# A transformer block with routed and shared experts: the shared network's operands fetched in the stage before, and its down products two chunks behind

## The chip, the cores and the metric

The kernel runs on one core of a Trainium2 chip. The metric is the device time of one execution, in microseconds (us); lower is better.

## What is computed

One block over x of 4 x 2048 tokens of width 256: attention, then a network of 8 routed experts (two for each token) beside a shared one. Everything is float32. The part that the change touches:

```python
y = jnp.einsum('te,etd->td', combine, expert_out)   # the two chosen experts, weighted
return y + _swiglu_mlp(identity, sw_gate, sw_up, sw_down)
# _swiglu_mlp: silu(x @ wg) * (x @ wu) @ wd, 256 -> 704 -> 256
```

and around it `x = x + gb * ffn(h)`, with h the normalized and modulated x (in the kernel: h2), and x itself before the addition (in the kernel: x1).

## The kernel before

The program is a row of stages, each with a block of instructions for every engine and a barrier at its end: setup, qkv, attention, middle (residual, norm, routing, rows scattered to the experts), expert, shared. The engines are TensorE (PE), VectorE (DVE), ScalarE (ACT), GpSimd (POOL) and SyncE (SP), which issues most DMAs; each works its list in order and waits on semaphores.

Products are made in fp32r with operands split in two: a high part (an ACT copy) and a low part (a subtraction, operand minus high part), and three products high-high, high-low, low-high.

**The expert stage** takes 39 blocks of 512 rows. For each it loads the expert's weights and the rows, transposes and splits them, makes three chunks of 128 hidden columns and adds them up in the down products; DVE copies the result (`take_made`, tile `made`, L1850) and SP stores it in `expert_made` (L1738). At its end SP waits for the last store.

**The shared stage** (`shared_stage`) loads the shared weights in five DMAs (L2008 to L2012), splits them (ACT L2096, DVE L2174), then walks 16 units of 512 tokens, unrolled. A unit has six chunks (NC = 6) of hidden columns; the sixth holds 64 columns of gate and, in the same product, 64 of up. For chunk i:

- PE: `up` (L2191) makes gate and up products, 12 matmuls of 512 columns, 6 for the last chunk. It needs the silu and `hid_f` of chunk i-2, whose PSUM it takes over. Then `down` (L2202), 12 matmuls of 256 columns, for the chunk before.
- ACT: silu (`act_g`, L2086, L2088). Behind that of chunk 2, `high_rows` of the next unit (`h_high`, L2077), which waits for its DMAs.
- DVE: `hidden`, three steps: `hid_f` (L2129), `hid_high` (L2133), `hid_low` (L2135). `finish` of the unit before stands behind chunk 0 (`total` L2147, `gated` L2150), `low_rows` of the next unit behind chunk 2 (`h_low`, L2140), `mix_experts` behind chunk 3 (`first` L2114, `mix` L2120).
- POOL: eight gathers of expert results for the next unit (`got`, L2051), then `y_out` = gated + x1 (L2064).
- SP: the loads of h2 and x1 for the next unit (L2017, L2019), which wait until `y_out` of the unit before is made, and the store of `y_out` (L2028).

The traces name the tiles of h2 `h` and those of x1 `x`; `in_done` counts both loads. `ps_d` has two buffers, `hid` has three (GS = 3), all else in the unit has two.

```python
pe.wait_ge(h2_done, u + 3)
for i in range(NC):
    up(u, i, slot)
    if i > 0:
        down(u, i - 1, slot)
    elif not (first and slot == 0):
        down(u - 1, NC - 1, 1 - slot)
```

`stand_alone` adds one to a semaphore that nobody waits for.

## Time and profile before

| | us |
|---|---|
| median of 3 runs | 3309.3 (3305.76 to 3310.84) |
| the profiled execution | 3308.82 |
| its span, first to last instruction | 3307.1 |
| PE busy in the span | 2912.5 (88%) |
| DVE busy | 2518.0 (76%) |
| ACT busy | 1588.5 (48%) |
| POOL busy | 884.5 (27%) |

Shares of busy time are means over stages that differ. PE's work of the expert stage, but for its first chunk, runs from 2304.6 to 2830.4 us of the span, and that of the shared stage from 2853.1 to 3298.8. Matmuls are pipelined: one of 512 columns is shown as some 0.39 us long and follows the last after 0.23. The end of a matmul is modelled.

### The profile page before, as it was taken

To read this page: it belongs to the slowest core of one execution; us is meant where nothing else is said; L and a number is where in the kernel's file an instruction comes from. 1 tells how busy PE (TensorE), PEld (TensorE's weight loads), DVE (VectorE), ACT (ScalarE), POOL (GpSimd) and SP (SyncE) were. 2 spreads that over 40 slices of the span, in tenths; PEclk is the share of its full clock that TensorE was granted. 3 is DMA by queue.
4 is the path that set the end of the run, shared out by engine and by line. 5 is a ranking of instruction groups with operands and counts; after the bars stand their busy time and mean duration, and the time that the engine had idled before them with its cause. 6 is when DMAs were issued, how large, how long until landed. Compare 5 with 4: busy or idle time off the path is not lost. (4 is left out here: it accounts for less than half of the span.)

```text
span 3307.1 us, 61435 instructions
## 1 busy us (share of the span) xinstructions
PE 2912.5 (88%) x22508; PEld 1616.0 (49%) x22508; DVE 2518.0 (76%) x4678; ACT 1588.5 (48%) x2160; POOL 884.5 (27%) x1100
## 2 busy tenths in 40 slices
PE   6885699999999999999999996873999999788888
PEld 3553133333333333333333325763888888677776
DVE  5885989888898888898888914664777777566665
ACT  2542166666676666666666782221444444111111
POOL 5773010111110111101111112664222222333332
PEclk8997699999999999999999997775999999899999
DMA  4776111122111212111221005664444455332332
GB/s 132 204 209 186 49 35 47 48 54 53 43 44 49 54 48 57 38 46 48 55 52 43 20 8 160 212 198 167 155 155 155 156 159 156 105 94 85 96 97 73
DMA packets 388533, 317.93 MB, mean 96 GB/s; under 512 B 112720, under 2 KB 374844, under 8 KB 388288
## 3 DMA queue, kind: packets, MB, share of 16 engines
q1 hardware_dynamic: 370752, 277.67, 29.4%
q0 software_dynamic: 12288, 33.57, 3.0%
q10 hardware_dynamic: 5248, 3.41, 0.4%
q8 instruction: 155, 2.54, 0.3%
q14 instruction: 90, 0.74, 0.1%
HBM read 196.89 MB, written 116.93 MB: 95 GB/s over the span
## 5 line engine op out<-in xcount | busy, mean ns | idle before, releaser
L903 ACT ACTIVATE probs<-ps_s 128x1024 f32<-128x1024 f32 (+3 forms) x1280 | 1077.9, 896 | 599.2 <-PE ps_s L1071 598.6
L926 DVE TENSOR_REDUCE piece_rest<-ps_m 128x1 f32<-128x512 f32 (+2 forms) x1260 | 748.8, 646 | 91.8 <-PE ps_m L1046 42.0
L1071 PE MATMUL ps_s<-q_st,k_st 50*128 50x512 bf16 (+7 forms) x5120 | 594.4, 346 | 19.0 <-ACT probs L903 15.2
L1086 PE MATMUL ps_o<-probs,vs 128*32 128x512 f32 (+3 forms) x5120 | 600.8, 541 | 4.3 <-POOL probs L883 1.2
L883 POOL TENSOR_SCALAR_AFFINE_SELECT probs<-probs 128x256 f32<-128x256 f32 x512 | 204.9, 406 | 1481.2 <-ACT probs L903 1476.0
L926 DVE TENSOR_REDUCE piece_late<-ps_m 128x1 f32<-128x512 f32 x900 | 548.8, 666 | 33.0 <-PE ps_m L1038 17.9
L1038 PE MATMUL ps_m<-k_st,q_st 48*128 48x512 bf16 (+3 forms) x2400 | 407.5, 353 | 65.8 <-DVE piece_rest L926 48.1
L1038 PEld LDWEIGHTS ps_m<-k_st,q_st 48*128 48x128 bf16 x2400 | 106.9, 93 | 651.8 <-DVE piece_rest L926 339.0
L1071 PEld LDWEIGHTS ps_s<-q_st,k_st 50*128 50x128 bf16 (+1 forms) x5120 | 224.1, 95 | 250.8 <-ACT probs L903 91.0
L1803 ACT ACTIVATE act_g<-ps_g 128x512 f32<-128x512 f32 x117 | 69.9, 597 | 279.5 <-PE ps_u L1895 279.5
L1840 DVE TENSOR_TENSOR hid_f<-act_g,ps_u 128x512 f32<-128x512 f32 x117 | 80.5, 688 | 126.8 <-ACT act_g L1803 126.8
L1086 PEld LDWEIGHTS ps_o<-probs,vs 128*32 128x32 f32 x5120 | 101.2, 108 | 142.8 <-issue 96.9
L2086 ACT ACTIVATE act_g<-ps_g 128x512 f32<-128x512 f32 x80 | 47.5, 595 | 251.1 <-PE ps_u L2191 206.3
L1765 POOL TENSOR_TENSOR wu_low<-wu,wu_high 128x768 fp32r<-128x768 f32 x39 | 76.8, 1968 | 326.1 <-ACT wu_high L1791 326.1
L2202 PE MATMUL ps_d<-sd_high,hid_high 128*128 128x256 f32 x384 | 114.0, 297 | 47.5 <-DVE hid_low L2135 46.2
L1359 POOL DMA_INDIRECT expert_rows<-rows,at x128 | 133.3, 1041 | 66.9 <-issue 36.0
L1845 DVE TENSOR_TENSOR hid_low<-hid_f,hid_high 128x512 fp32r<-128x512 f32 x117 | 138.8, 1187 | 4.0
L2051 POOL DMA_INDIRECT got<-expert_made,at_now x128 | 128.7, 1006 | 49.1 <-issue 36.8
L1907 PE MATMUL ps_d<-wd_high,hid_high 128*128 128x256 f32 x468 | 136.0, 291 | 1.2 <-DVE hid_low L1845 1.2
L1907 PE MATMUL ps_d<-wd_low,hid_high 128*128 128x256 f32 x468 | 132.1, 282 | 0.0
L1907 PE MATMUL ps_d<-wd_high,hid_low 128*128 128x256 f32 x468 | 132.0, 282 | 0.0
L621 PE MATMUL ps_qk<-wqkv,h_t 128*128 128x512 f32 x256 | 122.8, 603 | 1.0 <-ACT h_t L559 1.0
(228 smaller groups left out, 5103.2 us busy)
## 6 DMA issues: line engine op xcount, KB each, us to landing
k_st<-qk_parts SPq DMA_DIRECT2D x768, 32.0 KB, 1.8
qk_parts<-parts SPq DMA_DIRECT2D x124, 192.0 KB, 2.9
q_st<-qk_parts SPq DMA_DIRECT2D x720, 32.0 KB, 1.8
x_r<-expert_rows SPq DMA_DIRECT2D x39, 512.0 KB, 4.6
expert_made<-made SPq DMA_DIRECT2D x39, 512.0 KB, 2.9
x_in<-in_L_attn_x_dram SPq DMA_DIRECT2D x32, 512.0 KB, 4.7
vs<-v_ones SPq DMA_DIRECT2D x64, 256.0 KB, 3.7
v_ones<-v_out SPq DMA_DIRECT2D x60, 256.0 KB, 4.7
```

Of the source, the lines that this page charges most:

```text
L621: pe.matmul(ps_qk[:, t % 2, :], h_t[:, slot, c, t * P:(t + 1) * P], wqkv[:, c, 0:QK], start=(c == 0), stop=(c == DC - 1))
L883: pool.affine_select(out=block_now, in_=block_now, compare_op=ALU.is_ge, fill=0.0, base=0, pattern=[[0, 2], [1, P]], channel_multiplier=-1 ...
L903: act.activation(probs[:, u % PSLOTS, 2 * pair:2 * pair + 2, j * P:ST], ps_s[:, pair, :, j * P:ST], ACT.Exp, scale=SCALE).then_inc(exp_don ...
L926: v.tensor_reduce(dst, ps_m[:, bank, 0:n * w].rearrange("p (n w) -> p n w", n=n), AX.X, ALU.max) \
L1038: last[z] = pe.matmul(bank[:, i * w:(i + 1) * w], q_st[rows, slot, 0, a + i, qi * P:(qi + 1) * P], k_st[rows, slot, 0, a + i, kt * ST:kt * ...
L1071: last = pe.matmul(ps_s[:, pair, z, j * P:ST], k_st[rows, slot, half, pair, kc * P:(kc + 1) * P], q_st[rows, slot, half, pair, qt * ST + j ...
L1086: last = pe.matmul(ps_o[h * VW:(h + 1) * VW, j * P:ST], vs[:, slot, kc, h * VW:(h + 1) * VW], probs[:, u % PSLOTS, h, j * P:ST], start=(kc ...
L1359: pool.indirect_dma_start(rows_dram, bass.IndirectOffsetOnAxis(at[:, rslot, j:j + 1], 0), rows[:, rslot, j % TPS, :], None).then_inc(scatt ...
L1845: v.tensor_tensor(hid[1][:, i, :], hid_f[:, half, :], hid[0][:, i, :], ALU.subtract).then_inc(hid_done, 1)
L1907: last = pe.matmul(ps_d[:, t, :], hid[a][:, i, t * P:(t + 1) * P], wd_p[b][:, slot, i, :], start=(i == 0 and t % 2 == 0 and k == 0), stop= ...
L2051: pool.indirect_dma_start(got[:, slot, j, :], None, made_dram, bass.IndirectOffsetOnAxis(at_now[:, slot, j:j + 1], 0)) \
L2202: last = pe.matmul(ps_d[:, slot, t, :], hid[a][:, i % GS, t * P:(t + 1) * P], wd_p[b][:, i, :], start=(i == 0 and t % 2 == 0 and k == 0), ...
```

## The change

- The SBUF tiles of the shared weights and of h2, and of their parts, are made before the expert stage and live through both stages.
- In the expert stage SP loads the shared weights and h2 of unit 0 behind the loads of blocks 0 and 1. Behind the last block's work ACT makes the high parts (sg, su, h2, sd), DVE the low parts of sg and su ahead of `made` and that of h2 behind it, POOL that of sd.
- In the shared stage h2 has a semaphore of its own and is loaded two units ahead of its use in products, that is one unit earlier than before; its split moves behind chunk 0 (ACT) and chunk 1 (DVE).
- `down` follows two chunks behind `up` (LAG = 2), `finish` stands behind chunk 2.
- The `stand_alone` increments of the middle and shared stages go.

```diff
@@ constants
+SNC = -(-FS // P)
+SFULL = FS // P
+SHALF = FS - SFULL * P
@@ block_kernel
-        expert_stage(nc, C, rows_dram, made_dram, w_gate, w_up, w_down)
-        shared_stage(nc, C, h2_dram, x1_dram, made_dram, sw_gate, sw_up, sw_down, out_flat)
+        with ExitStack() as last:
...
+            W = dict(
+                wg=late("sg_w", [P, DC, SNC * P]), wu=late("su_w", [P, DC, SFULL * P]), wd=late("sd_w", [P, SNC, D]),
+                wg_p=[late(f"sg_{part}", [P, DC, SNC * P], F32R) for part in PARTS],
+                wu_p=[late(f"su_{part}", [P, DC, SFULL * P], F32R) for part in PARTS],
+                wd_p=[late(f"sd_{part}", [P, SNC, D], F32R) for part in PARTS],
+                h2=late("h2_5", [P, 2, DC, ST]),
+                h2_p=[late(f"h2_{part}", [P, 2, DC, ST], F32R) for part in PARTS],
+            )
+            expert_stage(nc, C, W, rows_dram, made_dram, w_gate, w_up, w_down, h2_dram, sw_gate, sw_up, sw_down)
+            shared_stage(nc, C, W, h2_dram, x1_dram, made_dram, out_flat)
@@ middle_stage: the same line goes at four places (Pool twice, Vector twice)
-                stand_alone(pool, held)
@@ expert_stage, SP, after the loads of blocks 0 and 1
+            sp.wait_ge(padded, 4)
+            wg_s, wu_s, wd_s = W["wg"], W["wu"], W["wd"]
+            up_cols = sw_up.rearrange("(c p) f -> p c f", p=P)
+            sp.dma_start(wg_s[:, :, 0:FS], sw_gate.rearrange("(c p) f -> p c f", p=P)).then_inc(next_in, 16)
+            sp.dma_start(wg_s[:, :, FS:SNC * P], up_cols[:, :, SFULL * P:FS]).then_inc(next_in, 16)
+            sp.dma_start(wu_s[:, :, :], up_cols[:, :, 0:SFULL * P]).then_inc(next_in, 16)
+            sp.dma_start(wd_s[:, 0:SFULL, :], sw_down[0:SFULL * P, :].rearrange("(j p) n -> p j n", p=P)).then_inc(next_in, 16)
+            sp.dma_start(wd_s[P - SHALF:P, SFULL, :], sw_down[SFULL * P:FS, :]).then_inc(next_in, 16)
+            sp.dma_start(W["h2"][:, 0, :, :].rearrange("p c t -> p (c t)"), h2_dram[0:P, :]).then_inc(next_in, 16)
@@ expert_stage, Pool, start and end
+            pool.memset(W["wd"][0:P - SHALF, SFULL, :], 0.0).then_inc(padded, 1)
+            pool.wait_ge(padded, 4)
...
+            pool.wait_ge(next_high, 4)
+            pool.tensor_tensor(W["wd_p"][1][:, :, :], W["wd"][:, :, :], W["wd_p"][0][:, :, :], ALU.subtract)
@@ expert_stage, Scalar, end
+            act.wait_ge(next_in, 16 * NEXT_DMAS)
+            for src, dst in ((W["wg"], W["wg_p"]), (W["wu"], W["wu_p"])):
+                act.activation(dst[0][:, :, :], src[:, :, :], ACT.Copy).then_inc(next_high, 1)
+            act.activation(W["h2_p"][0][:, 0, :, :], W["h2"][:, 0, :, :], ACT.Copy).then_inc(next_high, 1)
+            act.activation(W["wd_p"][0][:, :, :], W["wd"][:, :, :], ACT.Copy).then_inc(next_high, 1)
@@ expert_stage, Vector, end
+            for k, (src, dst) in enumerate(((W["wg"], W["wg_p"]), (W["wu"], W["wu_p"]))):
+                v.wait_ge(next_high, k + 1)
+                v.tensor_tensor(dst[1][:, :, :], src[:, :, :], dst[0][:, :, :], ALU.subtract)
             take_made(NB - 1, 0, NB // 2)
+            v.wait_ge(next_high, 3)
+            v.tensor_tensor(W["h2_p"][1][:, 0, :, :], W["h2"][:, 0, :, :], W["h2_p"][0][:, 0, :, :], ALU.subtract)
@@ shared_stage, SP (the five weight loads at its head go too)
-            def load(u, slot):
+            def load_h2(u, slot):
                 sp.wait_ge(h2_done, u + 1)
+                sp.dma_start(h2[:, slot, :, :].rearrange("p c t -> p (c t)"), h2_dram[ds(u * P, P), :]) \
+                    .then_inc(h2_in[slot], 16)
+
+            def load_x1(u, slot):
                 sp.wait_ge(out_done, u + 1)
-                sp.dma_start(h2[:, slot, :, :].rearrange("p c t -> p (c t)"), h2_dram[ds(u * P, P), :]) \
-                    .then_inc(in_done[slot], 16)
                 sp.dma_start(x1[:, slot, :, :], x1_dram[ds(u * ST, ST), :].rearrange("(t p) d -> p t d", p=P)) \
-                    .then_inc(in_done[slot], 16)
+                    .then_inc(x1_in[slot], 16)
...
                     if not (last and slot):
-                        load(u + 1, 1 - slot)
+                        load_x1(u + 1, 1 - slot)
+                    if not last:
+                        load_h2(u + 2, slot)
                     sp.wait_ge(out_done, u + 1 + 2)
...
-            load(0, 0)
+            sp.sem_inc(h2_in[0], 16)
+            load_h2(1, 1)
+            load_x1(0, 0)
@@ shared_stage, Pool (the memset of wd and two stand_alone go too)
-                    pool.wait_ge(in_done[slot], it * 32 + 32)
+                    pool.wait_ge(x1_in[slot], it * 16 + 16)
@@ shared_stage, Scalar
-                act.wait_ge(in_done[slot], turn_no * 32)
+                act.wait_ge(h2_in[slot], turn_no * 16)
...
-                        if i == 2 and not (last and slot):
+                        if i == 0 and not (last and slot):
                             high_rows(u + 1, 1 - slot, it + (1 + slot))
...
-            act.wait_ge(w_in, 16 * W_DMAS)
-            act.wait_ge(padded, 1)
-            for src, dst in ((wg, wg_p), (wu, wu_p), (wd, wd_p)):
-                act.activation(dst[0][:, :, :], src[:, :, :], ACT.Copy).then_inc(w_high, 1)
-            high_rows(0, 0, 1)
+            act.sem_inc(h2_high, 1)
@@ shared_stage, Vector
-            v.sem_inc(h2_done, 2)
+            v.sem_inc(h2_done, 3)
...
-                        if i == 0 and not (first and slot == 0):
+                        if i == LAG and not (first and slot == 0):
                             finish(u - 1, 1 - slot)
-                        if i == 0 and slot == 0:
+                        if i == LAG and slot == 0:
...
-                        if i == 2 and not (last and slot):
+                        if i == 1 and not (last and slot):
                             low_rows(u + 1, 1 - slot)
...
-            for k, (src, dst) in enumerate(((wg, wg_p), (wu, wu_p), (wd, wd_p))):
-                v.wait_ge(w_high, k + 1)
-                v.tensor_tensor(dst[1][:, :, :], src[:, :, :], dst[0][:, :, :], ALU.subtract).then_inc(w_done, 1)
-            low_rows(0, 0)
@@ shared_stage, Tensor (LAG = 2 is set at the stage's head)
                         up(u, i, slot)
-                        if i > 0:
-                            down(u, i - 1, slot)
+                        if i >= LAG:
+                            down(u, i - LAG, slot)
                         elif not (first and slot == 0):
-                            down(u - 1, NC - 1, 1 - slot)
...
-            pe.wait_ge(w_done, 3)
...
-            down(NST - 1, NC - 1, 1)
+            for i in range(NC - LAG, NC):
+                down(NST - 1, i, 1)
```

The instructions in order, in three places.

On DVE, where the expert stage ends and the shared one begins. `sg`, `su` and `sd` are the shared network's gate, up and down weights, `h_5` is h2, and high and low are their two parts. Before:

```order
L1843 CAST hid_high<-hid_f 128x512 [waits p4_down,p4_product]
L1845 TENSOR_TENSOR hid_low<-hid_f,hid_high 128x512 [waits p4_hid_high]
L1850 COPY made<-ps_d 128x1024 [waits p4_stored0,p4_down]
L1656 UNCONDITIONAL_BRANCH
L2102 UNCONDITIONAL_BRANCH [waits barrier_Pool_Activation_PE_DVE_SP_release]
L2174 TENSOR_TENSOR sg_low<-sg_w,sg_high 128x1536 [waits p5_w_high]
L2174 TENSOR_TENSOR su_low<-su_w,su_high 128x1280 [waits p5_w_high]
L2174 TENSOR_TENSOR sd_low<-sd_w,sd_high 128x1536 [waits p5_w_high]
L2140 TENSOR_TENSOR h_low<-h_5,h_high 128x1024 [waits p5_h2_high]
L2129 TENSOR_TENSOR hid_f<-act_g,ps_u 128x512 [waits p5_hid,p5_silu]
```

And now:

```order
L1874 CAST hid_high<-hid_f 128x512 [waits p4_down,p4_product]
L1876 TENSOR_TENSOR hid_low<-hid_f,hid_high 128x512 [waits p4_hid_high]
L1902 TENSOR_TENSOR sg_low<-sg_w,sg_high 128x1536 [waits p4_next_high]
L1902 TENSOR_TENSOR su_low<-su_w,su_high 128x1280 [waits p4_next_high]
L1881 COPY made<-ps_d 128x1024 [waits p4_stored0,p4_down]
L1905 TENSOR_TENSOR h_low<-h_5,h_high 128x1024 [waits p4_next_high]
L1666 UNCONDITIONAL_BRANCH
L2119 UNCONDITIONAL_BRANCH [waits barrier_Pool_Activation_PE_DVE_SP_release]
L2146 TENSOR_TENSOR hid_f<-act_g,ps_u 128x512 [waits p5_hid,p5_silu]
```

The three subtractions of weights and rows on DVE now stand ahead of the branch into the next stage, two of them ahead of the copy `made`; the one of sd is on POOL.

On SP, in the first units of the shared stage. Before:

```order
L2012 DMA sd_w<-in_L_ffn_sw_down_dram 64x256
L2017 DMA h_5<-h_t 128x1024 [waits p5_out,p5_h2]
L2019 DMA x_5<-x_mid 128x4x256
L2017 DMA h_5<-h_t 128x1024 [waits p5_out,p5_h2]
L2019 DMA x_5<-x_mid 128x4x256
L2028 DMA out_dram<-y_out 128x4x256 [waits p5_out]
L2017 DMA h_5<-h_t 128x1024 [waits p5_out,p5_h2]
L2019 DMA x_5<-x_mid 128x4x256
```

And now:

```order
L2031 UNCONDITIONAL_BRANCH [waits barrier_Pool_Activation_PE_DVE_SP_release]
L2035 DMA h_5<-h_t 128x1024 [waits p5_h2]
L2040 DMA x_5<-x_mid 128x4x256 [waits p5_out] x2
L2035 DMA h_5<-h_t 128x1024 [waits p5_h2]
L2051 DMA out_dram<-y_out 128x4x256 [waits p5_out]
L2040 DMA x_5<-x_mid 128x4x256 [waits p5_out]
L2035 DMA h_5<-h_t 128x1024 [waits p5_h2]
```

The load of h2 has come behind that of x1, is for one unit later, and waits for `p5_h2` alone.

On TensorE, the first unit of the shared stage; `ps_d` are down products, and the rows between are left out. Before:

```order
L2191 MATMUL ps_g<-h_high,sg_high 128x512 [waits p5_silu,p5_product,p5_h2,p5_w]
...
L2191 MATMUL ps_u<-h_high,su_high 128x512
...
L2191 MATMUL ps_g<-h_high,sg_high 128x512 [waits p5_product,p5_silu]
...
L2191 MATMUL ps_u<-h_high,su_high 128x512
...
L2202 MATMUL ps_d<-sd_high,hid_high 128x256 [waits p5_hid,p5_summed]
...
L2191 MATMUL ps_g<-h_high,sg_high 128x512 [waits p5_product,p5_silu]
```

And now:

```order
L2204 MATMUL ps_g<-h_high,sg_high 128x512 [waits p5_product,p5_silu,p5_h2]
...
L2204 MATMUL ps_u<-h_high,su_high 128x512
...
L2204 MATMUL ps_g<-h_high,sg_high 128x512 [waits p5_product,p5_silu]
...
L2204 MATMUL ps_u<-h_high,su_high 128x512
...
L2204 MATMUL ps_g<-h_high,sg_high 128x512 [waits p5_product,p5_silu]
...
L2204 MATMUL ps_u<-h_high,su_high 128x512
...
L2215 MATMUL ps_d<-sd_high,hid_high 128x256 [waits p5_hid,p5_summed]
```

The first down product stood behind two chunks of gate and up products, and stands behind three now.

## Rows read from the trace of the kernel before

**Rows 1.** three stretches: length, busy us of PE, PEld, DVE, ACT, POOL, granted clock, DMA

```profile
2304.60:2830.40 525.80, 524.62 (x3089) 456.85 (x3088) 392.52 (x500) 217.15 (x324) 149.82 (x76) 1.00 0.47 148
2853.10:3298.80 445.70, 398.07 (x2208) 336.99 (x2208) 295.14 (x478) 71.36 (x111) 157.81 (x146) 0.98 0.28 86
2853.00:2881.00 28.00, 27.70 (x139) 23.37 (x140) 14.90 (x30) 4.53 (x7) 4.76 (x5) 0.92 0.10 30
```

**Rows 2.** waits of the shared stage: who waited for whom, us in total, times, longest

```profile
PE ps_d L2202 <- DVE hid_low L2135: 46.2, 43, 3.2
```

**Rows 3.** timeline between the stages: start, us, engine, line, tiles, [idle before <-releaser]

```profile
2830.42 1.23 DVE L1850 COPY made<-ps_d 128x1024 f32<-128x1024 f32 x1 [1.79 <-PE ps_d L1907]
...
2831.67 0.37 SPq L1738 DMA_DIRECT2D expert_made<-made  x1
...
2835.00 0.39 SPq L2008 DMA_DIRECT2D sg_w<-in_L_ffn_sw_gate_dram  x1
...
2845.54 1.48 ACT L2096 ACTIVATE sg_high<-sg_w 128x1536 fp32r<-128x1536 f32 x1 [18.81 <-DMA sd_w<-in_L_ffn_sw_down_dram]
...
2847.05 1.76 DVE L2174 TENSOR_TENSOR sg_low<-sg_w,sg_high 128x1536 fp32r<-128x1536 f32 x1 [15.41 <-issue]
...
2851.80 1.22 DVE L2140 TENSOR_TENSOR h_low<-h,h_high 128x1024 fp32r<-128x1024 f32 x1
...
2853.12 0.76 PE L2191 MATMUL ps_g<-h_high,sg_high 128*128 128x512 f32 x1 [22.73 <-DVE h_low L2140]
```

**Rows 4.** timeline of one unit of the shared stage

```profile
3110.17 2.39 POOL L2064 TENSOR_TENSOR y_out<-gated,x 128x1024 f32<-128x1024 f32 x1 [13.90 <-issue]
...
3113.07 0.46 SPq L2017 DMA_DIRECT2D h<-h_t  x1
...
3119.32 1.06 ACT L2077 ACTIVATE h_high<-h 128x1024 fp32r<-128x1024 f32 x1 [5.27 <-DMA x<-x_mid]
...
3123.54 0.39 PE L2202 MATMUL ps_d<-sd_high,hid_high 128*128 128x256 f32 x1 [1.35 <-DVE hid_low L2135]
...
3128.15 0.39 PE L2202 MATMUL ps_d<-sd_high,hid_high 128*128 128x256 f32 x1 [1.59 <-DVE hid_low L2135]
```

**Rows 5.** the chain that ended last: start, us, engine, tile, line, instructions

```profile
2853.12 2.90 PE ps_g L2191 x6
...
3100.71 1.64 PE ps_d L2202 x12
...
3105.10 1.42 PE ps_d L2202 x12
...
3106.51 1.39 PE ps_g L2191 x6
...
3107.90 1.36 PE ps_u L2191 x6
```

**Rows 6.** timeline, DVE at the expert stage's last chunk

```profile
2826.76 0.69 DVE L1840 TENSOR_TENSOR hid_f<-act_g,ps_u 128x512 f32<-128x512 f32 x1 [2.30 <-ACT act_g L1803]
...
2827.94 0.69 DVE L1845 TENSOR_TENSOR hid_low<-hid_f,hid_high 128x512 fp32r<-128x512 f32 x1
```

**Rows 7.** timeline, POOL and DVE side by side in the expert stage

```profile
2801.29 1.97 POOL L1769 TENSOR_TENSOR wd_low<-wd,wd_high 128x768 fp32r<-128x768 f32 x1 [1.39 <-ACT wd_high L1794]
2801.60 2.21 DVE L1845 TENSOR_TENSOR hid_low<-hid_f,hid_high 128x512 fp32r<-128x512 f32 x1
```

**Rows 8.** groups of instructions (busy us, mean ns | idle), one gather in the timeline

```profile
L2051 POOL DMA_INDIRECT got<-expert_made,at_now x128 | 128.7, 1006 | 49.1 <-issue 36.8
...
L2120 DVE SCALAR_TENSOR_TENSOR mix<-got,weight_now,first 128x256 f32<-128x256 f32 x64 | 26.8, 479 | 0.6
...
2847.53 2.13 POOL L2051 DMA_INDIRECT got<-expert_made,at_now  x1 [0.81 <-issue]
```

**Rows 9.** timeline, SP and ACT at the start of the expert stage

```profile
2297.33 0.35 SPq L1721 DMA_DIRECT2D wg<-in_L_ffn_w_gate_dram  x1
...
2319.86 0.84 ACT L1791 ACTIVATE wg_high<-wg 128x768 fp32r<-128x768 f32 x1 [0.83 <-PE ps_d L1907]
```

More of the change, by code:

```diff
@@ L156, in block_kernel, with late @@
                      steps_dram, plan_dram)
-        expert_stage(nc, C, rows_dram, made_dram, w_gate, w_up, w_down)
-        shared_stage(nc, C, h2_dram, x1_dram, made_dram, sw_gate, sw_up, sw_down, out_flat)
+        with ExitStack() as last:
+            def late(name, shape, dt=F32):
+                return last.enter_context(nc.sbuf_tensor(name, shape, dt))
+            W = dict(
[8 more added lines that the diff above has]
+            shared_stage(nc, C, W, h2_dram, x1_dram, made_dram, out_flat)
 def stand_alone(eng, held):
@@ L1238, in middle_stage @@
         ps_r, ps_all = ps_rank[:, 0:TPS, :], ps_rank[:, TPS, :]
-        held = sem("p3_held")
         consts = sem("p3_consts")
@@ L1365, in run @@
                     pool.wait_ge(stat_done, u + 2)
-                    stand_alone(pool, held)
                     pool.tensor_scalar(var[:, :], mv[:, :, 1], EPS, None, ALU.add).then_inc(pool_own, 1)
@@ L1429, in statistics @@
                 v.wait_ge(dve_own, u + 1)
-                stand_alone(v, held)
                 for t in range(TPS):
@@ L1496, in choose @@
                 step(last)
-                stand_alone(v, held)
                 for t in range(TPS):
@@ L1644, in _, with expert_stage @@
             steps_of(run, pe)
-def expert_stage(nc, C, rows_dram, made_dram, w_gate, w_up, w_down):
+def expert_stage(nc, C, W, rows_dram, made_dram, w_gate, w_up, w_down, h2_dram, sw_gate, sw_up, sw_down):
     NC = -(-F // P)
@@ L1691, in expert_stage @@
         padded = sem("p4_padded")
+        next_in = sem("p4_next_in")
+        next_high = sem("p4_next_high")
+        NEXT_DMAS = 6
         w_high = sem("p4_w_high")
@@ L1929, in _, with shared_stage @@
             down(NB - 1, NC - 1, 0)
-def shared_stage(nc, C, h2_dram, x1_dram, made_dram, sw_gate, sw_up, sw_down, out_flat):
+def shared_stage(nc, C, W, h2_dram, x1_dram, made_dram, out_flat):
     NC = -(-FS // P)
@@ L1940, in shared_stage @@
     GS = 3
+    LAG = 2
     PICKS = TOPK * TPS
@@ L1952, in shared_stage @@
         gb, weight, made_at = C["gb"], C["weight"], C["made_at"]
-        wg = sb("sg_w", [P, DC, NC * P])
-        wu = sb("su_w", [P, DC, full * P])
-        wd = sb("sd_w", [P, NC, D])
-        wg_p = [sb(f"sg_{part}", [P, DC, NC * P], F32R) for part in PARTS]
-        wu_p = [sb(f"su_{part}", [P, DC, full * P], F32R) for part in PARTS]
-        wd_p = [sb(f"sd_{part}", [P, NC, D], F32R) for part in PARTS]
-        h2_p = [sb(f"h2_{part}", [P, 2, DC, ST], F32R) for part in PARTS]
-        h2 = sb("h2_5", [P, 2, DC, ST])
+        wg_p, wu_p, wd_p, h2, h2_p = (W[k] for k in ("wg_p", "wu_p", "wd_p", "h2", "h2_p"))
         x1 = sb("x1_5", [P, 2, TPS, D])
@@ L1977, in shared_stage @@
         ps_d = ps("ps_d5", [P, 2, TPS, D])
-        held = sem("p5_held")
-        padded = sem("p5_padded")
-        w_in = sem("p5_weights")
-        w_high = sem("p5_w_high")
-        w_done = sem("p5_w")
         h2_high = sem("p5_h2_high")
@@ L1987, in shared_stage @@
         hid_high = sem("p5_hid_high")
-        in_done = [sem(f"p5_in{i}") for i in range(2)]
+        h2_in = [sem(f"p5_h2_in{i}") for i in range(2)]
+        x1_in = [sem(f"p5_x1_in{i}") for i in range(2)]
         at_copied = sem("p5_at")
@@ L2001, in shared_stage @@
         stored = sem("p5_stored")
-        W_DMAS = 5
         block = ctx.enter_context(nc.Block())
@@ L2038, in _ @@
         def _(pool):
-            pool.memset(wd[0:P - HALF_CHUNK, full, :], 0.0).then_inc(padded, 1)
-            pool.wait_ge(padded, 1)
             pool.sem_inc(out_done, 2)
@@ L2044, in gather @@
                 pool.wait_ge(got_used, u + 1)
-                stand_alone(pool, held)
                 pool.tensor_copy(at_now[:, slot, :].rearrange("p (i t) -> p i t", i=TOPK),
@@ L2048, in gather @@
                 pool.wait_ge(at_copied, u + 1)
-                stand_alone(pool, held)
                 for j in range(PICKS):
@@ L2212, in body @@
                         up(u, i, slot)
-                        if i > 0:
-                            down(u, i - 1, slot)
+                        if i >= LAG:
+                            down(u, i - LAG, slot)
                         elif not (first and slot == 0):
-                            down(u - 1, NC - 1, 1 - slot)
-            pe.wait_ge(w_done, 3)
+                            down(u - 1, NC + i - LAG, 1 - slot)
             body(0, True)
```

5 lines of the change are left out of this document (removed).

## The prediction

> **What bounds the kernel now.** I read the busy totals by stage first, then the waits of the last stage, then single instructions where two stages meet and inside one unit. In the expert stage TensorE (PE) is busy 524.62 of 525.80 us at a granted clock of 1.00; in the shared stage it is busy 398.07 of 445.70 us [rows 1]. So the expert stage has nothing to give, while the shared stage has idle PE time, and so has the gap between the two. The waits say for what: before the down products PE waited 46.2 us in 43 places for DVE's `hid_low` [rows 2], and before the first shared matmul it sat idle 22.73 us [rows 3]. VectorE (DVE) is busy 295.14 of 445.70 us [rows 1], 18.4 us for each of 16 units: late, not full.
>
> What makes it late shows inside a unit. POOL's `y_out` runs 3110.17 to 3112.56, then SP issues the loads of h2 (3113.07) and x1; ScalarE (ACT) waits 5.27 us for them with the next silu queued behind, and starts `h_high` at 3119.32; DVE's `h_low` needs that, the chunk queued behind it is late, and PE stands 1.35 and 1.59 us before two down products [rows 4]. The same place comes back every 27.44 us (3100.71 [rows 5] to 3128.15 [rows 4]).
>
> **Part 1: the gap.** Before, the stage ended with `made` (2830.42 + 1.23), its store at 2831.67 and the barrier; SP began the weight loads at 2835.00, ACT started splitting at 2845.54, DVE ended `h_low` at 2853.02 and PE began at 2853.12 [rows 3]. Loads and splits leave this path. What takes their place, with the same durations:
> - ACT's last silu is over when hid_f starts, 2826.76 [rows 6]. The four copies follow, the weights having landed long before: sg 1.48 [rows 3], su 5/6 of that, h2 1.06 (the `h_high` of [rows 4]), sd 1.48, each overlapping its predecessor by some 0.1, so sd is done at about 2831.6.
> - DVE ends the last `hid_low` at 2828.63 [rows 6]. `sg_low` 1.76 [rows 3] and `su_low` 5/6 of it now stand ahead of `made`: 2828.6 to 2831.7, so `made` ends at 2832.9 instead of 2831.65, 1.2 late. From the start of the store to the new stage took 3.33 [rows 3], so on this path it starts at 2836.2.
> - POOL splits sd from 2831.7. A 128x768 subtraction took 1.97 [rows 7], so 128x1536 takes some 3.9: to 2835.6. DVE's `h_low` comes up at 2832.9. The same rows show what happens then: a DVE subtraction between SBUF tiles that started 0.31 us after POOL's took 2.21 instead of 0.69 [rows 6] and ended 0.55 after POOL. So `h_low` (1.23) ends about 1.1 after POOL, at 2836.7, and is the last to end; with a barrier of some 0.2 and DVE's opening semaphore counts PE starts at about 2837.3.
>
> The gap gives 2853.1 - 2837.3 = **15.8 us**. Bounds: 16.5 if `h_low` is not held up, and 13 if POOL or PE's start lose 3 us more. The Trainium skill, "SBUF — State Buffer", section "SBUF: two separate sides", says the port pair shared by DVE and GpSimd is an exclusive lock that the first comer keeps for its whole instruction; without it the stage would start some 0.5 us sooner, with it the sum stands.
>
> **Part 2: the units.** The PE work of a unit is five chunks of 1.39 + 1.36, one half chunk of 1.39 and six down products of 1.42 [rows 5]: 13.75 + 1.39 + 8.52 = 23.66 us, against 27.44 now. Does anything else keep PE from 23.66? I walk one unit, 0 being its first matmul. The gate and up products of chunks 0 to 5 end at 2.8, 6.9, 11.1, 15.3, 19.5 and 22.2. A chunk's hid_f starts 0.8 later and its three DVE steps take 1.9 (2826.76 to 2828.63) [rows 6].
> - Down products two chunks behind: hid(i) is needed 7 to 8.4 us after chunk i's products end, where one chunk behind it was 2.8 to 4.2. The other tie is that PE needs hid_f of chunk i (it frees PSUM) before chunk i+2: 4.2 to 5.6 us after.
> - DVE, in order: hidden 0 at 3.6 to 5.5; hidden 1 to 9.6 and `h_low` to 10.9; hidden 2 to 13.8, then total and gated (same 128x1024 size as `h_low`, 1.23 each [rows 3]) to 16.2; POOL's `y_out` then runs to 18.7 and holds back the cast of hidden 3, which ends at 19.8; the four steps of first and the four of mix (0.48 each [rows 8]; with overlaps about 2.9 together) to 22.6; hid_f 4 by 23.3; hidden 5 to 26.2; the next hidden 0 is ready only at 27.2. PE wants hid_f 4 at 23.66. This is the tightest place, with 0.3 us to spare.
> - h2: SP issues it behind the store and x1, about 20.0; in [rows 4] x1 and h2 together had landed 6.25 us after h2's issue, so it is there at 26.3. ACT asks for it at 27.8, and the next silu is late only if it lands after 29.6.
>
> So I cost lateness at nothing beyond the 1.2 us (525.80 - 524.62) that PE lost in the whole expert stage under a similar load [rows 1], taken once. 16 x 23.66 = 378.6; the cold start stays: the window behind the gap has a granted clock of 0.92 over 28 us [rows 1], 2.2 us lost, since a gap of 7 us is still long (the waits of 3.2 us in [rows 2] are the longest mid-stage ones; I do not count on the clock being kept). The last two down products now trail the last chunk and wait for hid 5: 1.0. Together 383.0, against 445.7: **62.7 us**. Cleaner units can hardly give more: without the cold start, the tail and the 1.2 it is 67.1.
>
> **Part 3: what is added or dropped elsewhere, at nothing.** Six DMAs (2.6 MB) go out in the expert stage behind block 1's loads. Their issue, some 3 us, fits before 2297.33, when the next load before could start, since it waits for a slot to be free [rows 9]. In the gap 2.1 MB of weights were in by 2845.54, 10.5 us after 2835.00 [rows 3]; at that rate the new ones end near 2307 and block 2's data near 2313, and ACT takes them at 2319.86 [rows 9]: 6 us of cover, and every microsecond beyond it would be added. One POOL memset moves stages and semaphore increments are gone; between 0 and 1 us gained, taken as 0. The gathers issue as before: eight of 1.01 us with 0.3 between [rows 8], the last begun some 10.5 us into the stage and, if it lands as slowly as h2 did, in at 16.8; the first mix comes at 17.5.
>
> **Sum.** 15.8 + 62.7 = 78.5 off the profiled execution's 3308.8 (span 3307.1 and 1.7 around it) gives 3230.3; the median of the runs is 0.5 above that execution, so I forecast **3231 us**.
>
> **The rivals.**
> - *DVE becomes the second bound.* The 0.3 us before hid_f 4 is worked out from durations only. For it: DVE needs 18.4 of 23.66 us and `y_out` blocks it for about 2 in each unit. Against: 5 us per unit are left, so lateness cannot pile up. If each of 15 boundaries costs 1 to 2 us: 3246 to 3261.
> - *h2 still late.* It now stands last of three transfers on SP and shares the engines with the gathers. It needs over 9.6 us to land where 6.25 is seen [rows 4]. At 3 us more than that PE would lose about 1 us a unit: 3246.
> - *Gathers starve.* POOL's unit is 2.4 (`y_out`), 1.2 (indices) and eight gathers of 1.3: 14 us. One gather beside DVE's splits took 2.13 [rows 8]; even if all did, POOL would need 23.1, just under 23.66. It bounds the stage from 2.5 us a gather, and at 3.15 the whole gain is gone; at 2.8 the unit is 26.0 and the time 3268. The Trainium skill, "SBUF — State Buffer", section "SBUF: two separate sides", has a box on DVE operations holding up the descriptors that GpSimd writes, and gives 620 ns alone against 3100 ns beside a DVE copy; by that figure the kernel would be slower, an estimate that the 1.01 us mean does not bear out.
> - *PE starts late in the new stage.* PE had 22 us to reach its code, now some 7. SP began right at the barrier [rows 3], which speaks against. Up to 3 us: 3234. The Trainium skill, "Runtime: NRT & Kernel Launch", section "Instruction fetch mechanics", says a taken branch can force a fetch before execution goes on; no row here shows what PE pays.
> - *The early loads hold up block 2.* 3 to 10 us: 3234 to 3241.
> - *Slower: the clock.* If PE, after the gap, does not get back from 1.2 to 2.4 GHz for long, a unit takes up to twice its 23.66 us (six gate products took 2.90 right behind the gap and 1.39 later [rows 5]). From 4 of 16 units at the lower level the gain is gone; with 8 of them it is 3420. The expert stage speaks against it: clock 1.00 with PE idle for 1.2 us in all [rows 1]. PE idles less than now, so this is remote.
>
> **How the numbers follow.** Forecast 0.72, DVE bound 0.11, h2 late 0.05, gathers 0.03, late PE start 0.05, block 2 held up 0.02, clock 0.02. The low end is all bounds on the good side, 67.1 + 16.5 = 83.6 off: 3225, and 2 us for the semaphores and for execution scatter: 3223. The upper end takes in the late starts, h2 late and half of the DVE case: 3254. Only the clock and the far end of the gathers lie above 3302. Faster by over 0.2% (6.6 us, about what a measurement of this kernel can tell from no change) 0.97, within 0.01, slower 0.02.
>
> **What would show it.** Right: PE's gap near 7 us with DVE `h_low` or POOL `sd_low` last before it; units 23.7 us apart; the wait of down products for `hid_low` near zero but for the last one; ACT's `h_high` waiting for PE, not DMA; block 2 of the expert stage at its old time. Wrong: a gap over 10 us, a wait of a gate product for DVE's hid_f at each unit's start, `h_high` behind a DMA again, a gather above 2 us, or a granted clock below 1.00 beyond the first window.

## The result and the profile after

The changed kernel takes 3255.05 us (median of 4 runs, 3249.14 to 3256.62) against 3310.07 us before in the same session: a ratio of 0.9831, 95% interval [0.9813, 0.9848]. It is faster, by 55 us where 78.5 were forecast, and 1 us above the forecast's range of 3223 to 3254. The profiled execution took 3249.14 us with a span of 3247.4; against the profiled one before (3308.8, span 3307.1) that is 59.7 us, and the stages below are told in this pair.

The first view is busy time in the two last stages of the changed kernel, as [rows 1] (length, busy us of PE, PEld, DVE, ACT, POOL, granted clock, DMA):

```profile
2320.80:2846.60 525.80, 524.82 (x3085) 456.64 (x3083) 394.18 (x503) 219.00 (x326) 149.88 (x76) 1.00 0.49 152
2854.90:3239.10 384.20, 381.04 (x2208) 336.06 (x2208) 296.13 (x477) 72.04 (x111) 175.45 (x159) 0.99 0.34 107
```

The expert stage still fills PE in a stretch of the same length. PE's work of the shared stage lost 61.5 us of its stretch. PE is idle in it for 3.2 us where it was for 47.6, which is 44.5 of the 61.5; the other 17.0 are busy time of the same 2208 matmuls (a group of twelve down products behind a wait is shown as 1.64 us, one without as 1.42 [rows 5]). The wait of `ps_d` for `hid_low` [rows 2] fell from 46.2 us to 0.8, and the largest wait of PE is now the start of the stage itself:

```profile
PE ps_g L2204 <- DVEq L2123: 6.4, 1, 6.4
...
PE ps_d L2215 <- DVE hid_low L2152: 0.8, 2, 0.6
```

Between the stages, in the timeline, as [rows 3]:

```profile
2846.04 0.69 DVE L1876 TENSOR_TENSOR hid_low<-hid_f,hid_high 128x512 fp32r<-128x512 f32 x1
...
2849.72 1.22 DVE L1881 COPY made<-ps_d 128x1024 f32<-128x1024 f32 x1
2849.76 3.42 POOL L1801 TENSOR_TENSOR sd_low<-sd_w,sd_high 128x1536 fp32r<-128x1536 f32 x1 [14.79 <-ACT sd_high L1846]
2850.85 3.40 DVE L1905 TENSOR_TENSOR h_low<-h,h_high 128x1024 fp32r<-128x1024 f32 x1
...
2854.86 0.77 PE L2204 MATMUL ps_g<-h_high,sg_high 128*128 128x512 f32 x1 [6.38 <-DVEq L2123]
```

Counted from the end of the last `hid_low` (2846.73): `made` ends at +4.2, POOL's `sd_low` at +6.5, `h_low` at +7.5, PE starts at +8.1. PE's gap is 6.38 us instead of 22.73. Inside the shared stage POOL's `y_out` comes back every 23.60 us:

```profile
3109.47 2.53 POOL L2085 TENSOR_TENSOR y_out<-gated,x 128x1024 f32<-128x1024 f32 x1 [10.04 <-issue]
...
3133.07 2.40 POOL L2085 TENSOR_TENSOR y_out<-gated,x 128x1024 f32<-128x1024 f32 x1 [10.03 <-issue]
```

So both parts that were costed came out. What is missing was lost in a stage that the forecast never looked at, the middle stage (attention's projection, routing, and the scatter of rows to the experts). Its length from the start of POOL's last setup memsets (`count`, at 1999.25 before, at 1997.79 after) to the first memset of the expert stage (2283.30, 2300.98), with the same view over just that stretch, before and after:

```profile
1999.30:2283.30 284.00, 200.41 (x1120) 169.57 (x1120) 167.36 (x766) 68.73 (x144) 154.26 (x164) 0.70 0.62 191
```

```profile
1997.80:2301.00 303.20, 209.60 (x1120) 178.23 (x1120) 166.57 (x766) 69.61 (x144) 149.18 (x165) 0.69 0.58 179
```

The same instructions take 19.1 us longer: with the same 1120 matmuls PE is busy 9.2 us longer and idle some 10 us longer. In the table a stage is counted from start to start (middle as above; expert from there to PE's first shared matmul; shared from there to the end of the span):

| stage | before | after | difference |
|---|---|---|---|
| up to the middle stage | 1999.3 | 1997.8 | -1.5 |
| middle | 284.0 | 303.2 | +19.1 |
| expert and gap | 569.8 | 553.9 | -15.9 |
| shared | 454.0 | 392.5 | -61.4 |

The change touches the middle stage in one way: four of its semaphore increments that stood alone (`stand_alone`) are gone, two on POOL (before the eight scatters of a unit, before `var`) and two on DVE (before the `mv` aggregates, before `which`). In a unit of the changed kernel (timeline, DVE's last index, POOL's first and last scatter, PE's transposes, ScalarE's two copies `h`, the routing products):

```profile
2099.27 0.17 DVE L1484 CAST at<-at_f 128x8 uint32<-128x8 f32 x1
...
2099.73 1.10 POOL L1372 DMA_INDIRECT expert_rows<-rows,at  x1 [1.95 <-DVE at L1484]
...
2108.04 1.04 PE L1621 MATMUL ps_h<-ident,rows 128*128 128x128 f32 x8
...
2108.72 0.96 POOL L1372 DMA_INDIRECT expert_rows<-rows,at  x1 [0.30 <-issue]
...
2109.77 0.60 ACT L1416 ACTIVATE h<-ps_h 128x512 f32<-128x512 f32 x1 [6.79 <-PE ps_h L1621]
...
2111.17 0.60 ACT L1416 ACTIVATE h<-ps_h 128x512 f32<-128x512 f32 x1 [0.80 <-remote]
...
2111.82 3.58 PE L1626 MATMUL ps_l<-gate_t,h 128*128 128x8 f32 x16 [2.74 <-ACT h L1416]
```

and the same of a unit of the kernel before:

```profile
2102.16 1.04 PE L1611 MATMUL ps_h<-ident,rows 128*128 128x128 f32 x8
...
2102.86 1.08 ACT L1404 ACTIVATE h<-ps_h 128x512 f32<-128x512 f32 x2 [6.97 <-PE ps_h L1611]
2103.09 0.96 POOL L1359 DMA_INDIRECT expert_rows<-rows,at  x1 [0.30 <-issue]
...
2104.00 1.95 PE L1616 MATMUL ps_l<-gate_t,h 128*128 128x8 f32 x16 [0.80 <-ACT h L1404]
...
2107.64 0.17 DVE L1473 CAST at<-at_f 128x8 uint32<-128x8 f32 x1
...
2108.66 1.10 POOL L1359 DMA_INDIRECT expert_rows<-rows,at  x1 [1.68 <-DVE at L1473]
```

Two things differ. The first scatter follows the start of `at` by 0.46 us after and by 1.02 before. And the two copies `h` start 1.40 us apart after, 0.49 before, although PE's transposes ran in one piece and the copy takes 0.60 both times. I call a pair over 0.9 us apart **late**. The changed kernel has 8 late pairs of 16, the kernel before none. This late pair costs twice: PE stands idle longer (2.74 against 0.80 us), and the clock then falls, as the windows of one microsecond of the changed kernel show (the granted clock is the third figure from the end):

```profile
2110.00:2111.00 1.00, 0.00 (x0) 0.00 (x0) 0.97 (x5) 0.37 (x1) 0.00 (x0) 1.00 0.37 131
2111.00:2112.00 1.00, 0.18 (x1) 0.18 (x2) 0.25 (x4) 0.60 (x1) 0.57 (x2) 0.73 0.00 0
2112.00:2113.00 1.00, 1.00 (x6) 1.00 (x6) 0.00 (x0) 0.00 (x0) 0.69 (x1) 0.50 0.41 164
```

so the routing products run at 0.50, which is 1.2 GHz, and take 3.58 us instead of 1.95 at 1.00.

### The profile page after: what moved, and what is told of

The parts are those of the page before. It is cut to its first block and busy times, and to the rows that moved or that the text cites. A ratio compares the mean times of both kernels' runs of the same rounds, so it can differ in the third digit from the quotient of the medians.

```text
span 3247.4 us, 61337 instructions
## 1 busy us (share of the span) xinstructions
PE 2902.9 (89%) x22508; PEld 1623.5 (50%) x22508; DVE 2519.7 (78%) x4677; ACT 1590.0 (49%) x2160; POOL 887.7 (27%) x1101
## 5 line engine op out<-in xcount | busy, mean ns | idle before, releaser
L1871 DVE TENSOR_TENSOR hid_f<-act_g,ps_u 128x512 f32<-128x512 f32 x117 | 80.5, 688 | 126.9 <-ACT act_g L1829 126.9
L2146 DVE TENSOR_TENSOR hid_f<-act_g,ps_u 128x512 f32<-128x512 f32 x80 | 54.8, 686 | 78.5 <-ACT act_g L2107 61.6
```

## The experiments: the middle stage

**All four increments back, two, or the kernel before without them.** To the changed kernel `e1_all_back` adds:

```
+        held = sem("p3_held")
...
+                stand_alone(pool, held)
                 for j in range(TOPK * TPS):
...
                     pool.wait_ge(stat_done, u + 2)
+                    stand_alone(pool, held)
...
                 v.wait_ge(dve_own, u + 1)
+                stand_alone(v, held)
...
                 step(last)
+                stand_alone(v, held)
```

> The changed kernel with the four semaphore increments of the middle stage put back (two on POOL, two on Vector). The trace of the changed kernel has a middle stage that is about 18 us longer (from the end of attention to the expert stage's first memset 316.8 us, before 297.3). Theory 'increments' (their removal is what costs): the middle stage is back at about 297 us and the kernel takes about 3237 us, ratio 0.978. Rival 'something else' (the length of the middle stage follows the placement of tiles and semaphores or the clock, not the increments): it stays near 3255 us, ratio 0.983.

Measured: 3237.39 us, ratio 0.9763 [0.9747, 0.9780]; middle stage 293.1 us, 2 late pairs.

`e2_pool_back` adds POOL's two alone, `e3_vector_back` DVE's two alone.

> The changed kernel with only POOL's two increments of the middle stage back. If POOL's order of waits before the first scatter of a unit matters: 3237 us as with all four, middle stage 297 us. If Vector's matter: 3255 us. If each has a part: between, and with the next run the two gains add up to that of all four.

> The changed kernel with only Vector's two increments of the middle stage back. If Vector's matter: 3237 us; if POOL's do: 3255 us. Under the rival that none of the four matters both this and the run before stay at 3255 us.

Measured: 3240.29 us (0.9775 [0.9758, 0.9791], middle 290.2, 1 late pair) with POOL's; 3254.45 us (0.9818 [0.9794, 0.9841], middle 307.3, 9 late) with DVE's. So POOL's matter and DVE's do not.

`e4_before_without` takes the four lines out of the kernel before.

> The kernel before with the four increments of the middle stage taken out and nothing else changed. Theory 'increments': the middle stage becomes about 18 us longer, so some 3328 us, ratio 1.0055. Rival 'something else' (another part of the change lengthens the middle stage): 3310 us, ratio 1.000.

Measured: 3332.52 us, ratio 1.0060 [1.0042, 1.0077]; middle 297.8 us in the profiled run, 6 late pairs. The loss is there without any other part of the change.

**Which of POOL's two, and what it does.** `e5_scatter_one` puts back the one before the scatters, `e6_var_one` the one before `var`, `e7_scatter_three` puts three in a row before the scatters, `e8_behind_scatter` one behind them. In `e7`:

```
                     pool.wait_ge(scattered[(rslot + 2) % RSLOTS], turn * SCATTER)
+                for _ in range(3):
+                    stand_alone(pool, held)
                 for j in range(TOPK * TPS):
```

> The changed kernel with one increment of the middle stage back: POOL's before the eight scatters of a unit. In the changed kernel's trace the scatters start 0.29 us behind the last index (Vector's `at`), with the increment 0.85 us; and in the units that are slow the two ScalarE copies `h` start 1.0 to 2.5 us apart instead of 0.49, while POOL's last scatter ended before or about the first copy. Theory 'phase' (the copies come late where the scatters end before them, so whatever holds the scatters back helps): about 3240 us, as with both of POOL's. Rival 'increment before the sum matters' (the one at `var`): 3255 us.

> The changed kernel with only POOL's increment before `var` back. Theory 'phase': the scatters still start 0.29 us behind the index, so it stays at about 3255 us, with some 8 to 10 of 16 pairs of copies `h` over 0.9 us apart. Rival 'the one at var': about 3240 us.

> The changed kernel with three increments in a row before the eight scatters, so that these start some 1 us or more later than with one. Theory 'phase': no pair of copies `h` over 0.9 us apart at all, middle stage at or under the 291 us of the kernel before, kernel about 3231 us. Rival 'a wait of its own' (what helps is that the wait stands in an instruction by itself, so one is enough and more only costs POOL's time): no better than with one, 3240 us or more.

> The changed kernel with one increment a unit behind the eight scatters instead of before them. Theory 'phase': the scatters are not held back, so it stays at about 3255 us, with 8 to 10 of 16 pairs of copies `h` over 0.9 us apart. Rival 'any increment on POOL does it': about 3240 us.

Measured: one before the scatters 3235.51 us (0.9771 [0.9755, 0.9787]), no late pair; before `var` 3254.35 (0.9827 [0.9811, 0.9843]), 8 late; three 3234.11 (0.9761 [0.9744, 0.9777]), none late; behind the scatters 3253.90 (0.9827 [0.9810, 0.9843]), 8 late. It is the place that matters: only what holds the scatters back helps. With the one increment the first scatter again follows `at` by 1.02 us, with three by 1.18, so the second and third hold it back by only 0.16 us more; the 1.4 us between the two times are inside the interval. With the hold one scatter of the unit also takes 1.86 us, as the timeline of `e5_scatter_one` has it:

```profile
2111.26 0.17 DVE L1486 CAST at<-at_f 128x8 uint32<-128x8 f32 x1
...
2112.28 1.10 POOL L1374 DMA_INDIRECT expert_rows<-rows,at  x1 [1.92 <-DVE at L1486]
...
2116.02 1.22 DVE L1455 TENSOR_TENSOR scaled<-xn,cb 128x1024 f32<-128x1024 f32 x1
...
2116.21 1.86 POOL L1374 DMA_INDIRECT expert_rows<-rows,at  x1 [0.30 <-issue]
...
2120.62 1.09 ACT L1418 ACTIVATE h<-ps_h 128x512 f32<-128x512 f32 x2 [5.65 <-PE ps_h L1623]
2120.91 0.96 POOL L1374 DMA_INDIRECT expert_rows<-rows,at  x1 [0.30 <-issue]
```

and in the unit of the changed kernel shown above the scatter beside the same DVE instruction:

```profile
2103.66 0.96 POOL L1372 DMA_INDIRECT expert_rows<-rows,at  x1 [0.30 <-issue]
...
2103.81 1.21 DVE L1453 TENSOR_TENSOR scaled<-xn,cb 128x1024 f32<-128x1024 f32 x1
```

The scatter that began 0.19 us behind `scaled` took 1.86 us, the one that began 0.15 us ahead of it 0.96. So with a hold of 0.56 us the last scatter of this unit ends 11.87 us behind the start of `at`, against 10.41 in the unit of the changed kernel: 1.46 us later.

**Is it the increment or the delay?** `e13_memset_short` and `e14_memset_long` have no increment, but a memset of a scratch tile in its place, 256 columns in the short one, 1024 in the long one:

```
                     pool.wait_ge(scattered[(rslot + 2) % RSLOTS], turn * SCATTER)
+                pool.memset(idle[:, rslot, 0:256], 0.0)
```

> The changed kernel, no increment back, but a POOL memset of a scratch tile (128x256) between the wait for the indices and the eight scatters. Theory 'delay' (the increment only holds the scatters back by some 0.6 us): this holds them back by about as much, so late pairs of copies `h` fall from 8 to 0 to 2 and the kernel takes about 3237 us. Rival 'the increment as such': 3255 us, some 8 late pairs.

> The same with a memset of 128x1024, about 1 us (the memset of `zeros` of that size takes 0.89 to 0.95 us). Theory 'delay': as with three increments, no or one late pair, about 3235 us. Rival 'the increment as such': 3255 us or more, since each unit pays 1 us on POOL.

Measured: 3240.05 us (0.9774 [0.9754, 0.9794]), 1 late pair; 3238.81 us (0.9777 [0.9759, 0.9794]), none. Either memset does it: the increment was a delay. The short one holds the scatters back by less than was expected, 0.72 us from `at` to the first scatter, the long one by 1.36:

```profile
2095.85 0.17 DVE L1486 CAST at<-at_f 128x8 uint32<-128x8 f32 x1
...
2096.08 0.31 POOL L1372 MEMSET idle<- 128x256 f32 x1 [1.11 <-DVE at L1486]
2096.57 1.10 POOL L1374 DMA_INDIRECT expert_rows<-rows,at  x1 [0.17 <-issue]
```

Over all runs: at 0.46 us there are 6 to 9 late pairs, at 0.72 one, at 1.02 (`before`, `e1`, `e2`, `e5`, `e15`) none to two, at 1.18 none (`e7`) and two (`e12`), at 1.36 none.

**More delay in the kernel before.** `e12_before_three` has three increments where the kernel before has one.

> The kernel before with three increments before the eight scatters of a unit instead of one, nothing else changed. Theory 'phase', from the changed kernel with three: the middle stage takes 285 us instead of 291, so about 3304 us, ratio 0.998. Rival 'only restores': the kernel before has no late pair of copies, so nothing is gained and each unit pays 1 us on POOL: 3310 us or more.

Measured: 3310.77 us, ratio 1.000 [0.9990, 1.0009]; middle 290.1 us with 2 late pairs. Nothing to gain, as the rival said, and a warning: two pairs are late here with the scatters held back by 0.16 us more, so a hold does not rule late pairs out. (The profiled run is the slowest of its ten.)

All profiled runs by their late pairs (middle stage in us):

| late pairs | middle stage |
|---|---|
| 0 | 284.1 (before), 284.0 (e15 below), 285.6 (e7), 287.6 (e14), 289.4 (e5) |
| 1 or 2 | 290.2 (e2), 291.3 (e13), 293.1 (e1), 290.1 (e12) |
| 6 | 297.8 (e4) |
| 8 | 303.2 (after), 304.9 (e6), 301.4 (e8), 307.4 (e9 below), 304.2 (e11 below) |
| 9 | 307.3 (e3), 300.2 (e10 below) |

From none (mean 286.1) to eight (mean 304.2) that is 2.3 us a late pair. It is a trend over single executions, and the five without a late pair differ by 5.4 us among themselves, for which no run gives a reason.

## The experiments: the shared stage

**The parts of the unit, one at a time.** `e9_one_behind` undoes the distance and keeps the h2 rows ahead:

```
-    LAG = 2
+    LAG = 1
...
-                        if i == LAG and not (first and slot == 0):
+                        if i == LAG - 1 and not (first and slot == 0):
...
-                        if i == LAG and slot == 0:
+                        if i == LAG - 1 and slot == 0:
```

> The changed kernel with the down products one chunk behind again (LAG 1, Vector's `finish` behind column 0), the h2 rows still a unit ahead. Theory 'h2 rows first' (a step model of the shared unit from the trace's durations: 27.6 us before, 23.6 with both, 24.3 with the h2 rows ahead alone): 15 units by 0.7 us, some 3265 us, and the waits of ps_d on hid_low come back, about 1.4 us each at the columns behind Vector's long work. Rival 'two behind is the larger part' (the 46.2 us of waits of ps_d in the kernel before were due to the distance alone): 3255 + 46 = 3301 us.

Measured: 3309.14 us, ratio 0.9993 [0.9976, 1.0010]; shared stage 452.3 us. My step model (24.3 us a unit) was wrong by far: the units are 26.4 to 28.2 us apart, and the h2 rows ahead alone bring the stage to about where it was before the change. In `e9` `total`, `gated`, hidden 1 and `h_low` follow one another in columns 0 and 1, and `y_out` holds up a cast in between (2.18 us instead of 0.43):

```profile
3007.69 1.22 DVE L2164 TENSOR_TENSOR total<-ps_d,mix 128x1024 f32<-128x1024 f32 x1
3008.94 1.22 DVE L2167 TENSOR_TENSOR gated<-total,gb_now 128x1024 f32<-128x1024 f32 x1
3010.08 0.68 DVE L2146 TENSOR_TENSOR hid_f<-act_g,ps_u 128x512 f32<-128x512 f32 x1
...
3010.80 2.18 DVE L2150 CAST hid_high<-hid_f 128x512 fp32r<-128x512 f32 x1
3013.01 0.69 DVE L2152 TENSOR_TENSOR hid_low<-hid_f,hid_high 128x512 fp32r<-128x512 f32 x1
3013.62 1.22 DVE L2157 TENSOR_TENSOR h_low<-h,h_high 128x1024 fp32r<-128x1024 f32 x1
```

The waits of the stretch 2880 to 3250 in `e9`, and in the kernel before:

```profile
PE ps_d L2215 <- DVE hid_low L2152: 36.1, 27, 3.6
```

```profile
PE ps_d L2202 <- DVE hid_low L2135: 41.6, 37, 3.2
```

`e10_h2_late` keeps the distance and loads h2 as before, with x1:

```
                 sp.wait_ge(h2_done, u + 1)
+                sp.wait_ge(out_done, u + 1)
                 sp.dma_start(h2[:, slot, :, :].rearrange("p c t -> p (c t)"), h2_dram[ds(u * P, P), :]) \
...
+                        load_h2(u + 1, 1 - slot)
                         load_x1(u + 1, 1 - slot)
-                    if not last:
-                        load_h2(u + 2, slot)
...
-            load_h2(1, 1)
```

with `h_high` and `h_low` back at column 2.

> The changed kernel with the h2 rows loaded as before (with the x1 rows, behind `y_out` of the unit before last; high and low parts at column 2), the down products still two chunks behind. Theory 'h2 rows first': with `finish` moved to column 2 the store of the output, and so the load, comes later than before, and the unit becomes longer than in the kernel before: the step model gives 33.4 us, 15 x 9.8 us more, some 3400 us. Rival 'the distance alone does it': the unit keeps its 23.6 us, 3255 us. Between them: 27.6 us a unit, 3315 us, if the load is only as late as before.

Measured: 3370.82 us, ratio 1.0189 [1.0167, 1.0212]; shared stage 511.2 us, units 31.5 to 32.6 us apart (33.4 in the step model). The distance alone makes the kernel slower than the one before, by 1.9%. The timeline of `e10` shows the ring: `finish` at column 2 makes `y_out` late, so the load, so `h_high`, and the chunks queued behind it on both engines:

```profile
3020.20 2.39 POOL L2084 TENSOR_TENSOR y_out<-gated,x 128x1024 f32<-128x1024 f32 x1 [18.45 <-issue]
...
3023.09 0.45 SPq L2036 DMA_DIRECT2D h<-h_t  x1
...
3027.78 1.06 ACT L2097 ACTIVATE h_high<-h 128x1024 fp32r<-128x1024 f32 x1 [12.02 <-DMA h<-h_t]
3028.87 1.22 DVE L2156 TENSOR_TENSOR h_low<-h,h_high 128x1024 fp32r<-128x1024 f32 x1 [8.80 <-ACT h_high L2097]
...
3030.83 0.76 PE L2203 MATMUL ps_g<-h_high,sg_high 128*128 128x512 f32 x1 [5.97 <-DVE hid_f L2145]
```

**Both undone.** `e11_early_only` has both diffs, so the early weights are what is left.

> The changed kernel with both parts of the shared unit undone (LAG 1, h2 rows loaded with the x1 rows), so that the weights loaded and split early and the increments' removal are all that is left of the change. If the early weights gain the 16 us that the gap between the stages shows and the middle stage costs its 18: unit 27.4 us as before, about 3310 - 16 + 18 = 3312 us, ratio 1.000. Rival 'the early weights cost the expert stage something': over 3316 us.

Measured: 3296.07 us, ratio 0.9960 [0.9946, 0.9973]. Expert stage and gap are 553.8 us, as in the changed kernel, so the early weights cost that stage nothing. But the shared stage took 440.7 us, 13 less than before. My expectation had left out one thing: h2 and x1 still land on semaphores of their own. (Two of POOL's increments are gone from the shared stage too, and no run puts them back.) `e15_before_split` makes only that split in the kernel before (with two of POOL's semaphores merged to make room):

```
-                    .then_inc(in_done[slot], 16)
+                    .then_inc(h2_in[slot], 16)
...
-                act.wait_ge(in_done[slot], turn_no * 32)
+                act.wait_ge(h2_in[slot], turn_no * 16)
```

> The kernel before, with the load of a unit's h2 rows and that of its x1 rows on semaphores of their own, so that ScalarE's h_high waits for the h2 rows alone (to make room for the semaphores two of POOL's own are merged into p5_held). With the two rearrangements of the shared unit undone, its stage took 440.7 us, the kernel before 454.0 us, and this split is what is left of the change there. Theory 'split': the shared stage takes about 441 us, the kernel 3297 us, ratio 0.996. Rival 'something else in that run' (the warm weights, the increments): 3310 us.

Measured: the profiled run has a shared stage of 442.1 us, as expected, and ScalarE's wait for the load is shorter; first the kernel before, then `e15` (2880 to 3250):

```profile
ACT h_high L2077 <- DMA x<-x_mid: 74.8, 13, 7.2
```

```profile
ACT h_high L2076 <- DMA h<-h_t: 45.2, 11, 4.7
```

But its ten runs lie between 3295.96 and 3310.51 us, median 3306.16, ratio 0.9974 [0.9962, 0.9985], and the profiled one, 3298.37, is the second fastest of them. So the split gains, 5 to 13 us by the interval; that it is all of the 13 us is not settled.

## Why the prediction was right in its parts and wrong in its sum

- **Part 1, the gap: right.** 15.9 us were gained from the start of the expert stage to PE's first shared matmul, forecast 15.8. From the end of the last `hid_low` the forecast had `made` at +4.3, POOL's start at +3.1, `h_low`'s end at +8.1 and PE at +8.7; measured +4.2, +3.0, +7.5 and +8.1. `sd_low` took 3.42 us where I took 3.9. DVE's `h_low`, started 1.09 us behind POOL's subtraction, took 3.40 us instead of 1.22 and ended 1.07 behind it (forecast 1.1). The exclusive lock of the Trainium skill, "SBUF — State Buffer", section "SBUF: two separate sides", agrees with that row.
- **Part 2, the units: right.** 23.60 us a unit, forecast 23.66, and 61.4 us for the stage, forecast 62.7. The walk through the unit held, the tightest place included: in the unit around 3110 hid_f 4 ends at 3116.52 and the next unit's first matmul starts at 3116.77, 0.25 us later where the forecast had 0.3. The load of h2 was nearer to being late than forecast: in the next unit `h_high` starts 7.6 us behind its issue, where 6.25 was counted, and stands 0.73 us behind its silu instead of 0.49; PE lost nothing by it. What was missed is a hole in the first unit, where PE waits for nothing that the profile shows:

```profile
2875.28 0.28 PE L2215 MATMUL ps_d<-sd_high,hid_high 128*128 128x256 f32 x1 [0.69 <-issue]
...
2876.00 0.28 PE L2215 MATMUL ps_d<-sd_high,hid_low 128*128 128x256 f32 x1 [0.31 <-issue]
2877.41 0.49 PE L2204 MATMUL ps_g<-h_high,sg_high 128*128 128x512 f32 x1 [1.13 <-issue]
2878.11 0.48 PE L2204 MATMUL ps_g<-h_low,sg_high 128*128 128x512 f32 x1 [0.21 <-issue]
```

  These are 2.3 us of the 3.2 that PE is idle in the stage. In the same way PE loses from 0.4 us (`e5`) to 4.3 (`e13`) there in the other kernels with the early weights, and nothing at that place in the kernel before; the cause stays open. That the sum still came within 1.2 us (384.2 against 383.0) is in part luck: the 1.2 us that was counted for lateness did not come, and the units were 1.0 us shorter in all.
- But Part 2 gave no sum for either rearrangement alone, and the runs show that apart each costs. With the split semaphores and neither of them the shared stage takes 440.7 us (`e11`); the rows ahead alone make it 452.3, the distance alone 511.2, both 392.5. It was the walk of the whole unit that got it right; the same model with one part taken out (`e9`) did not.
- **Part 3 failed**, at the step "semaphore increments are gone; between 0 and 1 us gained, taken as 0". It cost 19.1 us in the profiled pair, some 17 to 20 by the timed runs (3255.05 against 3237.39 and 3235.51 with the increment back; 3332.52 against 3315.36 without) and 20 to 23 by their ratios (0.9831 against 0.9763 and 0.9771; 1.0060). I costed the instruction, not what its delay did to the order in which POOL's scatters and ScalarE's copies fall, and I had no view of the middle stage at all. The other entries of Part 3 held: PE is as full in the expert stage as before, so no load delayed it, and the gathers neither starved nor lengthened the unit.
- No rival had it. All named places in the two last stages. A loss of 19 us put the time only 1 us outside the range because the range had been made wide for other reasons. With the increment before the scatters back, the forecast of 3231 stands against 3235.51 (one) and 3234.11 (three).

**The better version.** The changed kernel with that one increment (`e5_scatter_one`, 0.9771) or three (`e7_scatter_three`, 0.9761) is faster than both kernels compared here, by some 20 us against the change.

## What to carry to other kernels

An instruction that does nothing still takes a place in time; before dropping one in a loop, look at what runs right behind it and what that then runs beside, in every stage that the edit touches, not only in the stage that it is meant for. Two rearrangements of one pipeline should be costed together by a walk through the whole unit: here, in the shared stage and against the same kernel with neither, one alone lost 12 us, the other 70, and the pair gained 48. And one semaphore for two loads makes whoever needs the first wait for both; splitting it gained 5 to 13 us here.

## What was not expected of the hardware

- When POOL issues its scatters bears on how late ScalarE's copies start, though no data ties the two. In 6 of the 8 late pairs of the changed kernel POOL's last scatter had ended 0.04 to 0.31 us before the first copy; in the kernel before it ends 1.19 us or more behind it in every pair that has scatters beside it. Holding the first scatter back by 0.56 us leaves none to two late pairs. But in the other two of the changed kernel it ended 1.07 and 1.33 us behind the first copy, and `e12` has two late pairs with the end at 1.39 and 2.77: the order of the two makes late pairs likely, it does not explain each. Over all profiled executions the pair is late in 33 of 38 units where the last scatter had ended before the first copy, in 36 of 72 where it ended up to 1.5 us behind it, and in 1 of 128 where it ended later.
- Of the 70 late pairs of all profiled runs, 22 are 1.35 to 1.40 us apart. Through what the scatters reach a copy that waits only for PE stays open: PE's transposes are recorded as over 0.5 us and more before the second copy starts in each of these, and the profile gives PE's own event or a "remote" one as the releaser. Taking the scatters out of the stage altogether would have been the direct test and was not run, since the expert stage then has no rows to read.
- One increment that stands alone on POOL between a wait and an indirect DMA holds the DMA back by 0.56 us (1.02 against 0.46 us from `at` to the first scatter), but three in a row by only 0.72 (1.18).
- An indirect DMA issued by POOL took 1.86 us when it began 0.19 us behind DVE's 1.22 us `scaled`, and 0.96 when it began 0.15 us ahead of it (`e5` and the changed kernel): a shift of under half a microsecond decides which, and adds 0.90 us to the batch.
